# Token rows of u and v: eight TensorE transposes a pair replaced by one VectorE block transpose and sixteen SBUF transfers

## The reference

```
qz_u = xn @ u.T * SCALE          # 512 tokens x (16 heads x 64)
qz_v = xn @ v.T * SCALE
F    = einsum('bcsr,bctr->bcst', qz_u, qz_v)      # per head, 512 x 512
qh   = sigmoid(F)
qh_v1 = einsum('bcst,bctr->bcsr', qh, qz_v)
qh_v2 = einsum('bcst,bcsr->bctr', qh, qz_u)
message_G = (qh_v1 @ u + qh_v2 @ v) * SCALE
```

## Time and profile before

| | us |
|---|---|
| median of three runs | 1489.67 |
| the profiled execution, its own time | 1488.47 |
| its span, first to last instruction | 1486.7 |
| PE busy | 1439.0 |
| DVE busy | 832.9 |
| ACT busy | 753.3 |

### The profile page before, as it was taken

The page is one execution under the profiler, slowest core; times in us unless marked ns, Lnnn a source line. Parts: engine busy times, 40 slices in busy tenths (PEclk is TensorE's granted clock), DMA queues, the critical chain, the costliest instruction groups (busy, mean ns, idle before and its releaser), DMA issues.

```text
span 1486.7 us, 25056 instructions
## 1 busy us (share of the span) xinstructions
PE 1439.0 (97%) x8318; PEld 842.8 (57%) x8318; DVE 832.9 (56%) x1495; ACT 753.3 (51%) x1186; POOL 44.8 (3%) x41
## 2 busy tenths in 40 slices
PE   6989899999999999999999999999999999999978
PEld 2566555555655656556555555555655656555544
DVE  8868633455455554555555555555555554555547
ACT  3556556554545545455455554554445545455431
POOL 4000400000000000000000000000000000000000
PEclk9999999999999999999999999999999999999988
DMA  6012100000000000000000000000000000000000
GB/s 205 1 30 65 29 1 1 1 8 1 1 9 9 1 1 1 10 8 1 1 9 8 1 1 1 10 8 1 1 10 8 1 1 1 10 1 1 1 8 8
DMA packets 24090, 17.75 MB, mean 12 GB/s; under 512 B 2016, under 2 KB 22240, under 8 KB 23936
## 3 DMA queue, kind: packets, MB, share of 16 engines
q1 hardware_dynamic: 23600, 14.20, 3.6%
q0 software_dynamic: 336, 1.64, 0.3%
HBM read 11.64 MB, written 4.19 MB: 11 GB/s over the span
## 4 chain that ended last, share of the span: by engine, by line
issue 86%; DVE 1%; PE 1%; POOL 1%; ACT 0%; POOLq 0%; DVEq 0%
PE psum L1203 1%; DVE arena L881 0%; DVE arena L887 0%; DVE arena L879 0%; POOL v_w_hl L580 0%; POOL u_w_hl L580 0%; POOL rstd_s L595 0%; DVE arena L903 0%; PE psum L1555 0%; DVE xn_s L635 0%; POOL u_w_hl L577 0%; POOL v_w_hl L577 0%; POOL up_hl L580 0%; DVE x_all L896 0%; POOL gate_hl L577 0%
## 5 line engine op out<-in xcount | busy, mean ns | idle before, releaser
L1137 ACT ACTIVATE arena<-psum 128x1024 f32<-128x1024 f32 x504 | 475.6, 1030 | 591.5 <-PE psum L1203 574.5
L1203 PE MATMUL psum<-arena 128*64 128x512 f32 x2016 | 460.4, 598 | 0.0
L1203 PEld LDWEIGHTS psum<-arena 128*64 128x64 f32 x2016 | 133.5, 136 | 249.0 <-issue 245.4
L1203 PE MATMUL psum<-v_parts,u_parts 64*128 64x512 f32 (+1 forms) x1568 | 202.6, 398 | 2.4 <-DVE o_hl L832 2.4
L1203 PE MATMUL psum<-u_parts,v_parts 64*128 64x512 f32 x1536 | 196.2, 399 | 5.2 <-issue 4.4
L830 DVE TENSOR_SCALAR o_hl<-psum,sums 128x512 fp32r<-128x512 f32 x126 | 94.5, 750 | 183.9 <-PE psum L1203 183.8
L1203 PEld LDWEIGHTS psum<-v_parts,u_parts 64*128 64x128 f32 (+1 forms) x1568 | 145.1, 185 | 84.5 <-issue 51.1
L1203 PEld LDWEIGHTS psum<-u_parts,v_parts 64*128 64x128 f32 x1536 | 139.7, 184 | 85.6 <-issue 49.8
L986 ACT ACTIVATE arena<-psum 128x512 f32<-128x512 f32 (+3 forms) x186 | 104.3, 610 | 30.6 <-PE psum L1203 18.4
L832 DVE SCALAR_TENSOR_TENSOR o_hl<-psum,sums,o_hl 128x512 fp32r<-128x512 f32 x126 | 94.6, 751 | 4.5
L887 DVE TENSOR_TENSOR arena<-psum,arena 128x512 f32<-128x512 f32 x96 | 64.6, 689 | 49.8 <-PE psum L1203 47.9
(11 more groups left out here) (211 smaller groups left out, 1578.6 us busy)
## 6 DMA issues: line engine op xcount, KB each, us to landing
x_all<-in_x SPq DMA_DIRECT2D x4, 512.0 KB, 5.7
upper<-in_we SPq DMA_DIRECT2D x8, 256.0 KB, 2.7
expert_rows<-upper SPq DMA_DIRECT2D x16, 128.0 KB, 2.5
xn_s<-expert_rows SPq DMA_DIRECT2D x8, 256.0 KB, 2.8
out<-x_all SPq DMA_DIRECT2D x8, 256.0 KB, 2.9
arena<-in_e POOLq DMA_DIRECT2D x1, 896.0 KB, 5.1
arena<-in_wi POOLq DMA_DIRECT2D x1, 576.0 KB, 5.6
uT_w<-in_uT SPq DMA_DIRECT2D x1, 512.0 KB, 6.6
```

What stands on the lines that cost most here:

```text
L1137: nc.scalar.activation(th_of(un), psum[:, at:at + 2], ACT.Tanh, scale=0.5 * FACTOR_SCALE ** 2).then_inc(s_th, 2)
L1203: return nc.tensor.matmul(out, lhsT, rhs, start=start, stop=stop)
```

## The change

`tu` and `tv` are gone, on PE and on ACT. `u_raw` and `v_raw` now lie side by side, and at the end of each even half, after `evac_o` (and `add_y`, where one follows), DVE turns both in one operation (`turn`): every 32x32 block of the 128x1024 values is transposed in place of its block, into a buffer `blocks`. The blocks are then in the right orientation but in the wrong partitions. SP waits for it and issues 16 DMAs from SBUF to SBUF (`move_tokens`), one for each of 4x4 block rows: 32 partitions, 8 runs in each, 32 values (128 bytes) a run, 32 KB a DMA, 512 KB a pair. They write the token buffer that the next pair uses. PE's first `weighted` of a pair waits until all 16 have landed (16 x 16 = 256 counts of the semaphore, `MOVED`), DVE's `turn` waits for the same before it writes `blocks` again, and ACT's `prep_raw` waits for the turn before it writes `u_raw` again.

The diff, cut to its core:

```diff
-PREP_IN_HALF = [("pu", "pv", "pj"), ("tu", "tv")]
-PREP_K = {"pu": 1, "pv": 2, "tu": 3, "tv": 4}
+PREP_IN_HALF = [("pu", "pv", "pj"), ()]
+PREP_K = {"pu": 1, "pv": 2}
+QUARTERS = 4
+MOVED = 16 * QUARTERS * QUARTERS
...
-        u_raw, v_raw = take(T), take(T)
-        u_tok, v_tok = take(2, TB, P), take(2, TB, P)
+        raw = take(2, T)
+        v_raw, u_raw = raw[:, 0], raw[:, 1]
+        tok = take(2, 2 * TB * P).rearrange("p h (w k c) -> p h w k c", w=2, k=TB)
...
+            def move_tokens(i, j, blocks):
+                sp.wait_ge(s_turned, i * PAIRS + j + 1)
+                for r in range(QUARTERS):
+                    for a in range(QUARTERS):
+                        sp.dma_start(tok[32 * r:32 * r + 32, (j + 1) % 2, :, :, 32 * a:32 * a + 32].rearrange("t w k c -> t (w k) c"),
+                                     blocks[32 * a:32 * a + 32].rearrange("t w (k r c) -> t (w k) r c", k=TB, r=QUARTERS)[:, :, r])\
+                          .then_inc(s_moved[j], 16)
+            move_rows(E - 2, E // 2 - 1, 0)
+            move_tokens(0, 0, first_blocks)
+            move_rows(E - 1, E // 2 - 1, 1)
...
+            def batch(n, more):
+                for j in range(PAIRS):
+                    move_tokens(n, j, later_blocks)
+                    if j == 1 and more:
+                        sp.wait_ge(s_yp, n + 1)
+                        wait_emptied(sp, ("norm", 0), n - 1)
+                        load_rows(n + 1)
+                store(n - 1)
...
+            def turn(i, j, blocks):
+                if not (isinstance(i, int) and i == j == 0):
+                    dve.wait_ge(s_moved[(j - 1) % PAIRS], (i + (j > 0)) * MOVED)
+                nc.vector.transpose(blocks.rearrange("p w t -> p (w t)"), raw.rearrange("p w t -> p (w t)")).then_inc(s_turned, 1)
...
             prep_v(0, 1)
+            dve.wait_ge(s_prep_w, 1)
+            turn(0, 0, first_blocks)
             expert_rows(E - 1, 1, E // 2 - 1)
...
                         if second and Y_AT[r] == h:
                             add_y(r, i - 1)
+                    if o == 0:
+                        if not some_before:
+                            for n in range(2):
+                                dve.wait_ge(s_ymv[n], 16 * E)
+                        turn(i, j, later_blocks)
...
-                    act.wait_ge(s_prep_full, prep_index(g, 1))
+                    act.wait_ge(s_turned, g)
...
-            def prep_tok(g, k, tok, par, q, bk):
-                act.wait_ge(s_prep_full, prep_index(g, k) + 1)
-                if q is not None:
-                    act.wait_ge(s_out, (q - 1) * 8)
-                copy(tok[:, par].rearrange("p k c -> p (k c)"), bk[:]).then_inc(s_prep_free, 1)
...
-                    pe.wait_ge(s_prep_free, prep_index(g, k - 2) + 1)
-                    for t in range(TB):
-                        ins = nc.tensor.transpose(bk[:, t * P:(t + 1) * P], (u_raw if k == 3 else v_raw)[:, t * P:(t + 1) * P],
-                                                  ident[:])
...
                 if u == 0:
-                    pe.wait_ge(s_prep_free, prep_index(g - 1, 4) + 1)
+                    pe.wait_ge(s_moved[(j - 1) % PAIRS], (i + (j > 0)) * MOVED)
```

More of the change, by code:

```diff
@@ L157, in first_middle_of @@
 def first_middle_of(h):
-    work = [w for w in MIDDLE[h] if w[0] in ("pu", "pv", "pj", "tu", "tv") and w != ("pj", 1)]
+    work = [w for w in MIDDLE[h] if w[0] in ("pu", "pv", "pj") and w != ("pj", 1)]
     return work + [("sc", 0)] * (h == FIRST_SCATTER_HALF)
@@ L194, in is_prep @@
 def is_prep(work):
-    return work[0] in ("pu", "pv", "pj", "tu", "tv", "sc")
+    return work[0] in ("pu", "pv", "pj", "sc")
 def prep_index(g, k):
-    return g * 4 + 3 + k
+    return g * 2 + 3 + k
 def is_first(g):
@@ L370, in build @@
         w_hl = [u_w_hl, sb("v_w_hl", [P, 2, PAIRS * D], F32R)]
+        later_blocks = sb("blocks", [P, 2, T])
         def th_of(un):
@@ L407, in build @@
         s_us, s_vs_rdy = sem("u_parts_ready"), sem("v_parts_ready")
+        s_turned, s_moved = sem("blocks_turned"), [sem(f"tokens_moved{j}") for j in range(PAIRS)]
         s_f, s_th, s_out, s_oe = sem("scores_full"), sem("tanh_done"), sem("unit_done"), sem("o_evacuated")
@@ L519, in _ @@
                 move_rows(E - 4 + par, E // 2 - 2, par)
-            for par in range(2):
-                move_rows(E - 2 + par, E // 2 - 1, par)
+            def move_tokens(i, j, blocks):
[8 more added lines that the diff above has]
+            move_rows(E - 1, E // 2 - 1, 1)
             def load_rows(n):
@@ L532, in _ @@
             load_rows(0)
-            sp.wait_ge(s_yp, 1)
-            load_rows(1)
-            with sp.Fori(1, B - 1) as n:
[L536 to L540, removed]
+            for j in range(1, PAIRS):
+                move_tokens(0, j, later_blocks)
+                if j == 2:
+                    sp.wait_ge(s_yp, 1)
+                    load_rows(1)
+            def batch(n, more):
[6 more added lines that the diff above has]
+                store(n - 1)
+            with sp.Fori(1, B - 1) as n:
+                batch(n, True)
+            batch(B - 1, False)
             store(B - 1)
@@ L1186, in iteration @@
                             prep_raw(g, 2, v_raw, sums[:, 0], (j + 1) % 2, q, x_bank(work, second))
-                        elif work[0] == "tu":
-                            prep_tok(g, 3, u_tok, (j + 1) % 2, q, x_bank(work, second))
-                        elif work[0] == "tv":
-                            prep_tok(g, 4, v_tok, (j + 1) % 2, q, x_bank(work, second))
                         elif not is_prep(work) and second:
@@ L1444, in prep @@
                 pair = slice(j * P, (j + 1) * P)
-                if k in (1, 2) and is_first(g):
+                if is_first(g):
                     ins = mm(bk[:], (uT_w if k == 1 else vT_w)[:, pair], xn1T[:, 0])
-                elif k in (1, 2):
+                else:
                     if j == 0 and k == 1:
@@ L1454, in prep @@
                     ins = product(bk, uv_hl[k - 1], pair, xn1_hl)
-                else:
-                    pe.wait_ge(s_prep_free, prep_index(g, k - 2) + 1)
-                    for t in range(TB):
-                        ins = nc.tensor.transpose(bk[:, t * P:(t + 1) * P], (u_raw if k == 3 else v_raw)[:, t * P:(t + 1) * P],
-                                                  ident[:])
                 ins.then_inc(s_prep_full, 1)
```

15 lines of the change are left out of this document (5 added, 10 removed).

## The result

The changed kernel took 1465.97 us (median of 4 runs, 1462.72 to 1468.40), the kernel before 1488.88 in the same round (4 runs). The ratio is 0.9847, 95% interval 0.9834 to 0.9860: 1.5% faster. The forecast was 1444 us, so the sign and the range hold and about half of the gain is missing. The profiled execution took 1468.4 us with a span of 1466.6; before it was 1486.7, so 20.1 us of span have to be accounted for.

A forecast was written before the change was run, and what follows sets the result against it. PE's matmuls were taken to bound the loop, so removed transposes shorten it unless the replacing chain is late. -61.6 + 1 + 15 = -45.6 us from 1488.5 gives 1442.9, median 1444; forecast's range 1437 to 1475, 8 in 10 1430 to 1615.

The forecast's parts named there:

- the form of the chain: From PE's weighted of one even half to the next: evacuations, turn, 16 SP issues, last landing, handovers; 18.3 us, 18.9 with add_y.
- The chain's terms: Weighted and evacuations 5.24 us, turn 1.2, 16 issues 9.6, last landing 2.1, three semaphore handovers 0.2.
- fast issue: Rival: move issues on SP 0.44 us apart as for the store, no pair late, 1433 us; chance 0.21.
- slow issue: Rival: 32-partition move issues on SP 0.87 us apart, all pairs late, 1613 us; within the slower case's chance of 0.38.
- the issue term: SP's 16 move issues per pair, 0.64 us apart: 15 x 0.64 = 9.6 us from first to last.
- They are nearer to the first: The 32-partition moves resemble the 64-partition expert moves (0.64 us apart) more than the 128-partition store (0.44).
- the slower rival: The moves make PE late and the kernel slower than before, anywhere from 1493 us up; chance 0.38.
- Batch 0: The first batch, before the loop: 6 us for late pairs + 8.4 start - 2.4 earlier wait + 3 clock = 15 us lost.
- 56 x 1.1 = 61.6 us: Gain from removing PE's transposes: 1.1 us for each of 56 pairs in the loop's seven batches.
- such a shadow in batch 0: Batch 0's transposes lie beside weighted's wait for the third tanh, so removing them saves 0 there.
- the bounds 0.94 and 1.2: PE time of a pair's eight transposes: 0.94 us from start distances, 1.2 us from their summed durations; 1.1 was taken.
- only the last is late, by 0.2 us: Of the loop's eight pairs per batch, only the last is shorter than its chain: 7 x 0.2, about 1 us.

## Why the prediction was right, and where it was not

**What bounds the kernel, and the form of the chain: right.** PE waits at weighted of even halves for the landing of the moves. The prediction's "as long as nothing else becomes late" did not hold in one place: the idle time at the loop's branch grew from some 0.7 us a batch to 1.8.

**The chain's terms: right in size.** Evacuation, turn, distance, landing and handovers came to 18.17 us against 18.3. The turn was 1.234 us against 1.2. The estimate from the Trainium skill's "VectorE: DVE Perf Modes", "The three transpose paths" (eight times the 311 ns of a 16-bit piece, 2.5 us), is twice the measured 1.234; the plain pass over the values was the nearer row. The rivals of fast issue (0.44) and slow issue (0.87) both fell: the distance was 0.65.

**The reason for the issue term: wrong.** "They are nearer to the first" rested on the number of partitions. Single DMAs showed that this number plays no such part, and that SBUF on both sides does: 0.64 for the term and 0.65 for the measurement agree by luck. The same mistake made the slower rival look likely, with 0.38. The Trainium skill, "DMA: Bandwidth & Descriptors", "Issuing engines are not separate DMA queues", calls the sequencer's time usually small against the DMA; here 16 issues are 10.4 of a chain of 18.2 us and the landing of the last 2.

**Batch 0: right, +15.8 against +15.** The start was +8.3 (8.4 forecast). Three of the middle pairs lost 1.06 us each (18.16 against 17.10; 1.2 forecast), the last two 2.15 and 2.83 (the last behind a wait of 2.06 us, with the lower clock), and the first pair gained 0.6 instead of losing 0.6.

**The step that failed first: 56 x 1.1 = 61.6 us.** Loop batches without any wait are 157.7 us, so the transposes were worth 7.0 a batch, about 50 us in seven. Two things were missed. In the last odd half of a batch the transposes stood beside the tanh and the loop's branch, so that one pair in eight gives nothing. The prediction had seen such a shadow in batch 0 and had ruled it out for the loop by the second layer's work; in this half that work is 1.1 us of `wo` products, and the branch follows. The last batch, with no branch behind it, gave 7.8 us even with the moves in it. And of the bounds 0.94 and 1.2 the lower was the better for most others: five of the seven gave 0.86 to 1.02 us.

**The step that failed second: "only the last is late, by 0.2 us", about 1 us.** It was 13.7 us in six batches. Some 8 of them are the chain's. It was taken as a constant, and it has a tail: about one issue in 22 takes up to 1.9 us in place of 0.61. A single one was enough for the fourth pair, which had 0.2 us to spare in the prediction and waited in all six batches. Two of them in one pair made PE wait 2.28 us, with the lower clock for 3.4 us behind it. The prediction had written that the cover is thin and had not priced it. The kernel whose chain is 2.6 us shorter has as many long issues and no such wait. Another 4 us are the branch's: 3.4 for the clock behind it, twice, and 0.9 for its longer idle time. The prediction had no term for either, and a shorter chain does not remove them. Whether the moves make the branch slower (3.9 us in the mean, 3.8 with a quarter of them) stays open.

Together: -49.6 + 13.7 + 15.8 = -20.1 us, the measured difference of the spans; -45.6 had been forecast. About 12 us of the missing 25 are the first step and 13 the second.

## What to carry to other kernels

When work moves off the bounding engine onto a chain of DMA issues, count the issues and not the bytes: here one SBUF to SBUF issue came 0.65 to 0.72 us behind the other with 32 to 128 KB each, four of 16 done by an engine copy gave back 20 us, and the same bytes in 4 to 8 DMAs made PE wait only 1.9 us, at the start. Give the chain slack of a few us over the period that it must fit, because long issues (up to 1.9 us) come back at the same place of every batch, and a long wait can bring the lower clock. And ahead of a loop's end, look for the last wait and the branch behind it before a gain is counted there: what is saved turns into idle time of PE, and the clock can fall behind that too.

## What the runs showed of the hardware that was not expected

- A block transpose of 128x1024 float32 values on DVE takes 1.234 us, and 2.16 us if its output is written with a step of 32 bytes; a copy of 32x256 takes 0.28.
- An issue on SP takes 0.61 to 0.68 us for SBUF to SBUF with 32 to 128 partitions and 128-byte runs, and 0.52 to 0.59 with 1 KB runs. With DRAM at one side it takes 0.33 to 0.40, but 0.51 (a store) and 0.66 (a load) with 64 partitions.
- 16 KB instruction packets take 0.9 to 1.6 us, 44 of 46 long issues overlap one, and they come back at the same places of every batch.
- The branch back to the top of the loop takes PE's sequencer 3.4 to 4.3 us in the changed kernel and 3.5 to 3.9 in the one before, and begins only when the last wait ahead of it has ended. Idle times of 1.8 to 2.2 us behind it brought the lower clock in some batches and not in others.
